# A one-core decoder layer on Trainium2: TensorE's loop order, second SBUF buffers, matmuls ahead of the first weights, and new orders on every engine

## The reference

```python
# 16 heads of 16, 64 random features (orf)
phi(z)  = (exp(z @ orf.T / 2 - |z|^2 / 8) + 1e-6) / 8
a       = phi(q) @ (phi(k).T @ v) / (phi(q) @ sum(phi(k)))       # linear attention, q, k, v from x
x1      = LN(x + a @ Wo.T + bo)
x2      = LN(x1 + softmax(q' k'.T / 4) v')                       # q' from x1, k', v' from the context
gate,up = aq(x2) @ tern(w_gate).T, aq(x2) @ tern(w_up).T         # aq: rows rounded to 8 bits
out     = LN(x2 + aq(silu(gate) * up) @ tern(w_down).T)          # tern: weights rounded to three levels
```

## Time and profile before

| | us |
|---|---|
| median of 3 runs | 495.16 (495.1 to 498.17) |
| the profiled execution, its own time | 495.66 |
| its span, first to last instruction | 493.6 |
| PE busy | 447.2 (91% of the span) |
| DVE busy | 436.0 (88%) |
| ACT busy | 429.1 (87%) |
| POOL busy | 393.3 (80%) |
| mean granted clock of TensorE | 0.977 of full |

### The profile page before, as it was taken

One profiled execution on the slowest core, in us unless ns is written; L12 is line 12 of the kernel. 1 busy time (PEld: TensorE's weight loads), 2 busy tenths in 40 slices (PEclk: granted clock), 3 DMA queues, 4 the chain that ended last, 5 costly groups with the idle time before them and its releaser, 6 DMA issues.

```text
span 493.6 us, 18532 instructions
## 1 busy us (share of the span) xinstructions
PE 447.2 (91%) x6598; PEld 305.1 (62%) x6598; DVE 436.0 (88%) x1286; ACT 429.1 (87%) x879; POOL 393.3 (80%) x885
## 2 busy tenths in 40 slices
PE   5588898999999999999999999999999999878752
PEld 3345666777666766777767677766766666554321
DVE  7755568999999999999999999999999999898771
ACT  3398988999999999999999999999999999776632
POOL 3379677889997898999999999999999897764533
PEclk9889999999999999999999999999999999997997
DMA  7848667777787587566666666666667676542122
GB/s 206 263 109 140 124 120 110 132 134 140 142 142 140 121 150 143 116 140 148 140 142 139 143 143 139 144 149 149 145 130 136 118 140 141 97 76 56 42 55 64
DMA packets 192660, 64.27 MB, mean 130 GB/s; under 512 B 172385, under 2 KB 192353, under 8 KB 192609
## 3 DMA queue, kind: packets, MB, share of 16 engines
q1 hardware_dynamic: 192432, 63.60, 64.2%
q10 hardware_dynamic: 176, 0.01, 0.0%
HBM read 17.31 MB, written 4.19 MB: 44 GB/s over the span
## 4 chain that ended last, share of the span: by engine, by line
PE 58%; DMA 11%; ACT 10%; DVE 9%; issue 5%; POOL 3%; SPq 3%; POOLq 0%; DVEq 0%; ACTq 0%
PE bank L1355 10%; PE bank L1741 8%; DMA tT<-pkT 5%; PE bank L1682 4%; PE bank L1543 4%; PE bank L1780 4%; PE bank L1453 3%; PE bank L1500 2%; PE bank L1719 2%; PE bank L1387 2%; PE bank L1392 2%; DVE hh L1101 2%; DMA pkAT<-pkA 2%; PE bank L1515 2%; PE bank L1571 2%
## 5 line engine op out<-in xcount | busy, mean ns | idle before, releaser
L1355 PE MATMUL bank<-wq_hi,xT 128*128 128x512 f16 (+1 forms) x256 | 73.2, 341 | 1.5 <-ACT xT L636 1.5
L516 POOL TENSOR_TENSOR rs<-ve,mhalf 128x1 f32<-128x1 f32 x96 | 53.2, 555 | 0.0
L1052 DVE TENSOR_REDUCE negm<-bank 128x4 f16<-128x512 f32 x64 | 42.9, 670 | 6.7 <-PE bank L1592 6.6
L1097 DVE SCALAR_TENSOR_TENSOR g<-th,bank 128x512 f32<-128x512 f32 x64 | 43.0, 675 | 4.7 <-ACT th L774 3.5
L750 ACT ACTIVATE pT<-bank 128x512 f32<-128x512 f32 x64 | 39.0, 610 | 8.0 <-PE bank L1672 6.9
L1355 PE MATMUL bank<-wq_lo,xT 128*128 128x256 f16 (+1 forms) x128 | 43.5, 340 | 0.0
L1053 DVE TENSOR_REDUCE negm<-bank 128x4 f16<-128x512 f32 x64 | 43.5, 679 | 0.0
L682 ACT ACTIVATE x<-y,nmr,rs 128x256 f32<-128x256 f32 x64 | 39.8, 623 | 3.6 <-DVE y L1158 2.9
L702 ACT ACTIVATE phq<-bank 128x512 f32<-128x512 f32 x64 | 39.7, 637 | 3.2 <-PE bank L1387 3.2
L1101 DVE TENSOR_TENSOR hh<-g,bank 128x512 f32<-128x512 f32 x64 | 42.4, 674 | 0.0
L1780 PE MATMUL bank<-downT,hqT 128*128 128x256 bf16 x256 | 33.2, 273 | 8.1 <-DMA hqT<-hq 8.1
(11 more groups left out here) (186 smaller groups left out, 1570.0 us busy)
## 6 DMA issues: line engine op xcount, KB each, us to landing
xs<-in_x_dram SPq DMA_DIRECT2D x32, 128.0 KB, 2.3
xr<-in_x_dram SPq DMA_DIRECT2D x32, 128.0 KB, 2.3
cs<-in_ctx_dram SPq DMA_DIRECT2D x32, 128.0 KB, 2.2
out_dram<-ot SPq DMA_DIRECT2D x32, 128.0 KB, 2.0
ffn_ld<-in_L_ffn_w_gate_dram SPq DMA_DIRECT2D x1, 1024.0 KB, 8.9
ffn_ld<-in_L_ffn_w_up_dram SPq DMA_DIRECT2D x1, 1024.0 KB, 6.4
ffn_ld<-in_L_ffn_w_down_dram SPq DMA_DIRECT2D x1, 1024.0 KB, 8.4
pkAT<-pkA SPq DMA_TRANSPOSE x64, 3.2
```

The costliest lines, as they stand in the source:

```text
L516: g.tensor_tensor(rs[n - 1][:, :], ve[n - 1][:, :], mhalf[:, :], ALU.pow).then_inc(done[f"pw{n}"], 1)
L1052: v.tensor_reduce(negm[:, 0, cols], even.rearrange("p (c t) -> p c t", c=4), AX, ALU.max, negate=True)
L1097: v.scalar_tensor_tensor(g1[:, n, :], th[:, n, :], 1.0, gate, ALU.add, ALU.mult).then_inc(done[f"gl{n}"], 1)
L1355: last = T.matmul(o, xT[:, 2 * part + c, :], w[:, c, cols], start=(n == 0), stop=(n == 5))
```

## The change

- **Second buffers.** Eleven tiles (`xpk`, `xT`, `qk`, `pkA`, `pkAT`, `phk`, `x1T`, `pkT`, `pkC`, `hq`, `hqT`) get a dimension of two, indexed by parity. To make room `th` and `g1` are laid over `wld`. Waits that guarded the single buffers go: `hi` and `nhi` no longer wait for the transposes of the tile before, `qT`/`kT` no longer for `phq0`/`phk1` of the tile before, `qk_` not for `lo`, `xhi` not for `xTp`.
- **TensorE's loop order and the PSUM banks.** Both are new. `tm` goes to the end of the iteration with lag 4, `kvp` to near its start with lag 3, `phk0`, `phk1`, `ntp` behind `s0`, `wo` between `st0` and `nump`, `u1` beside `u0`. Waits for freed banks follow the new bank table.
- **Matmuls ahead of the weights.** 18 matmuls of 128 x 128 identity by identity before the first weight transposes, and 8 after the second.
- **Orders anew** on SP, POOL, ACT and DVE, in ramp, loop and drain. In the ramp, DVE's first `magnitude` comes after the first `qk_`, `v_` and `nr`; SP issues `w_up` and `w_down` ahead of `x[2]`; SP's loop has `tT_` last, right behind `load_c` and `load_r`. In the drain 43 unread matmuls stand in place of 32. DVE's clears of `pkA`, `pkC`, `pkT` cover only the rows that no step writes.

```diff
-        pkA = sb("pkA", [P, H, 4, 32], F16)
-        pkAT = sb("pkAT", [P, H, P], F16)
+        pkA = sb("pkA", [P, 2, H, 4, 32], F16)
+        pkAT = sb("pkAT", [P, 2, H, P], F16)
...
-        th = sb("th", [P, 2, 512])
-        g1 = sb("g1", [P, 2, 512])
+        th = wld[:, 0:2, :, :].rearrange("p a b d -> p a (b d)")
+        g1 = wld[:, 2:4, :, :].rearrange("p a b d -> p a (b d)")
...
             def qT(t, par):
-                wait_ahead(sp, t, par, ("lo", 0), ("phq0", -1))
+                wait_ahead(sp, t, par, ("nlo", 0))
...
             def nhi(t, par):
-                wait_ahead(pool, t, par, ("nr", 0), landings=(("kT", -1), ("qT", -1),))
+                wait_ahead(pool, t, par, ("nr", 0))
...
             def hi(t, par):
-                wait_moved(act, "kT", t, par, -1)
-                wait_moved(act, "qT", t, par, -1)
+                wait(act, "qk", t)
...
             def qk_(t, par):
                 wait(dve, "qkm", t)
-                wait(dve, "lo", t, -1)
...
+            def keep_busy(count):
+                for _ in range(count):
+                    T.matmul(at_qk[:, 0:P], idh[:, :], idh[:, :], start=True, stop=True)
+
+            keep_busy(18)
             for n in range(3):
                 transpose_weight(n, weight_banks[n])
+                if n == 1:
+                    keep_busy(8)
...
             def st0(t, par):
+                wait_looped(pe, "tlo", t, 1)
                 wait_looped(pe, "xT", t, 6)
```

More of the change, by code:

```diff
@@ L422, in drain @@
[L422 to L431 removed]
+                trail(tT_, i, -232, 25)
@@ L432, in _ @@
+                trail(qT, i, -235, 28)
+                trail(load_c, i, -235, 28)
+                trail(cT_, i, -233, 25)
+                trail(store, i, -226, 19)
+                trail(hqT_, i, -229, 21)
+                trail(load_r, i, -235, 27)
+                trail(row, i, -232, 24)
+                trail(load_x, i, -258, 30)
+                trail(kT, i, -236, 28)
+            run(sp, ramp, iteration, drain, (-219, -131), 18, 30, (-228, -194))
             for par in range(2):
@@ L880, in _ @@
+            run(act, ramp, iteration, drain, (-31, -16), 16, 30, (-20, -7))
         @block.vector
@@ L1285, in _ @@
+            run(dve, ramp, iteration, drain, (-29, -10), 14, 30, (2, 14))
         @block.tensor
@@ new lines, in ramp @@
+                once(ternaries[1], i, -27)
+                lead(dn, i, -23, 3)
+                lead(kvp, i, -29, 9)
+                if i == -25:
+                    pe.wait_ge(done["m1"], 2)
+                once(ternaries[4], i, -25)
+                lead(wo, i, -28, 8)
+                lead(st1, i, -26, 6)
+                lead(st0, i, -26, 6)
+                lead(nump, i, -29, 9)
+                lead(phk1, i, -30, 10)
+                lead(qkm, i, -32, 12)
+                lead(pv1, i, -26, 6)
@@ new lines, in ramp @@
+                lead(pv0, i, -26, 6)
+                lead(s0, i, -27, 7)
+                lead(phk0, i, -30, 10)
+                lead(ntp, i, -29, 9)
+                lead(xqTp, i, -25, 5)
+                once(output_weight, i, -31)
+                lead(oxp, i, -26, 6)
+                if i == -27:
+                    pe.wait_ge(done["nT"], 3)
+                once(ternaries[2], i, -27)
+                lead(phq1, i, -30, 10)
+                lead(phq0, i, -30, 10)
+                lead(s1, i, -27, 7)
@@ L1913, in _ @@
-            run(pe, ramp, iteration, drain, (-50, -12), 14, 30, (-6, 6))
+                trail(pv0, i, -43, 24)
+                trail(vm, i, -48, 30)
+                trail(s0, i, -44, 25)
+                trail(phk0, i, -47, 28)
+                trail(qkm, i, -49, 30)
+                trail(ntp, i, -46, 27)
+                trail(oxp, i, -43, 24)
+                trail(phq1, i, -47, 28)
+                trail(xqTp, i, -42, 23)
+                trail(s1, i, -44, 25)
+                trail(kvs, i, -47, 28)
@@ new lines, in drain @@
+                keep_busy_at(i, -12, 6)
+                trail(kvp, i, -47, 27)
+                trail(dn, i, -41, 21)
+                keep_busy_at(i, -11, 18)
+                keep_busy_at(i, -12, 13)
+                trail(st1, i, -44, 24)
+                trail(st0, i, -44, 24)
+                trail(wo, i, -46, 26)
+                trail(pv1, i, -44, 24)
+                trail(nump, i, -47, 27)
+                trail(xTp, i, -50, 30)
+                trail(phk1, i, -48, 28)
+            run(pe, ramp, iteration, drain, (-33, -19), 14, 30, (-20, -9))
```

1234 lines of the change are left out of this document (577 added, 657 removed), and 10 rows, old and new, of the table done.

## The result

The kernel after takes 503.48 us (median of 3 runs, 502.51 to 506.65), the kernel before 495.16. The ratio is 1.0156, 95% interval [1.0119, 1.0193]: slower by 1.6%, where I had forecast 483.8. The profiled execution took 502.51 us with a span of 500.8, 7.2 above that of before.

What follows compares the result with a forecast made beforehand. Chains of waits were taken to bound ramp and drain, work the loop (PE full, ACT and DVE close behind). -3.5 - 4.5 + 0 - 2.4 - 1 = -11.4 from 495.66 gave 484.3 us, 483.8 as a median; range 475 to 495.

Steps and rivals of the forecast that it cites:

- The start, -3.5: Before tile 0: `qk_` starts right behind its projection, not behind the gate's `magnitude`; -3.5 us, between -5 and 0.
- Second buffers in 20 to 80 us, -4.5: Ramp: the guards of the single `pkA` on DVE and POOL go; 4.5 us gained, a little under half of ACT's idle time.
- the sign "over 90%": Sign that the forecast is right: ACT over 90% busy in 20 to 80 us.
- 80 to 200 us, "nothing": Gain there put at nothing, engines being 95 to 97% busy; term 0, between -3 and +3 for late landings.
- cost nothing visible: Claim on SP's order, `hqT` buffers, aliases, added waits and clears; without cover, a tenth of a microsecond a tile.
- The loop, -2.4: Tile from 12.94 to 12.84 us by changes of shape and the `mTp` wait; over 24 tiles -2.4, between -7 and +7.
- hidden behind PE: In the loop the guards of the single buffers wait under 0.2 us a tile, covered by PE's work.
- the last rival: Changes of shape are no fewer, nine and nine; the 0.05 us a tile go, +1.2, 485.0; half the forecast's chance.
- SP, POOL, the rest: Remaining order changes each lie on an engine behind work it had to await anyway; no visible cost.
- The distance from `tm` to `s0`: Shrinks by 0.68 us, leaving 0.1 to 0.15; holds in the loop, late ramp landings cost up to 0.68 each.
- the slower rival: Loop: `s0` waits for the transpose each tile; at a 4.1 us landing +18 over 24 tiles, 505 us; chance 0.14.
- The drain, -1: After the loop: same chain, distance less 0.68, new orders may use second buffers; -1 us, between -5 and +4.

Runs made afterwards that it cites:

- e12_start: Kernel before with DVE's first magnitude moved from ahead of the first `qk_` to behind the first `nr`; ratio to the kernel before 0.9958.
- e11_guards: Kernel after with the waits of the single `pkA`, `pkAT` and `qk` put back for tiles 1 to 11; ratio to the kernel before 1.0378.
- e14_buffers: Kernel before with second buffers for `pkA`, `pkAT` and `qk` alone, its orders as they were; ratio to the kernel before 0.9977.
- e13_circle: Kernel after with `ya2` ahead of `chi` in POOL's loop and, in SP's ramp, `hqT_` ahead of `qT` and `store` behind `load_r`; ratio to before 1.0012.
- e1_ya2: Kernel after with `ya2` ahead of `chi` in POOL's loop; ratio to the kernel before 1.0077, a tile 12.96 us.
- e16_s0: e13_circle with `s0` behind `phk0` and `ntp` in TensorE's straight ramp, as it stood before; ratio to the kernel before 1.0073.
- e8_nobusy: Kernel after without the 18 and 8 matmuls ahead of the weights; ratio to the kernel before 1.0238.
- e17_split: e13_circle with `load_r` ahead of `row` and `load_c` behind `tT_` in SP's loop; ratio to the kernel before 1.0061, a tile 12.94 us.
- e6_loads: Kernel after with `load_c` and `load_r` ahead of `row` in SP's loop; ratio to the kernel before 1.0144, a tile 13.29 us.
- e5_qT: Kernel after with `qT` behind `hqT_` and `row` in SP's straight ramp, as before; ratio to the kernel before 1.0174.

## Why the prediction was wrong

*The start, -3.5.* Tile 0 was 4.1 us earlier, at 11.7, and its projection ran at twice the pace. Right in place and size; e12_start shows that only about 2 us of such a gain reach the end.

*Second buffers in 20 to 80 us, -4.5.* Start and ramp together gave 5.9 of the 8.0 by tile 7. In the new orders the guards are worth even more than the term (e11_guards: 6.4 us), but the buffers own only half of it: alone they give nothing there (e14_buffers). ACT's share rose hardly, 50.34 us against 50.05; the sign "over 90%" did not come.

*80 to 200 us, "nothing".* This step failed, by 7.8 us from tile 7 to 17, where the range went to +3. I let the gain of the ramp be lost against engines that are full, and bounded the rest by the late landings at `s0`, 0.68 us each. I had read SP's order only for its last entry. What failed, as far as it is known, is that I put the rest of SP's new order under "cost nothing visible": with `qT` ahead of `hqT_` in the ramp, SP's own issue time, 1.25 us a transpose, entered a circle of 13.3 us. Mending it together with `store` gives 3.2 us by the ratios, 2.7 of them between tiles 7 and 17 in the traces (e13_circle against e1_ya2). That is less than half: the other 6.0 us of this stretch, 2.8 in tiles 8 and 9 and 2.5 in tile 12, stay open. The late landings are real, but before had them too, and giving the distance back in the ramp does not help (e16_s0). Part of it may be an early ramp that is lost again, for which my sum has no term; that is not shown, but e8_nobusy and e11_guards reach tile 7 3.6 and 6.4 us later than the kernel after and tile 17 only 1.2 and 4.2 later.

*The loop, -2.4.* The second failed step, +4.2 from tile 17 to 29. Without its stalls TensorE's own order takes 12.7 us against my 12.84. But the order has little part in that: with the second buffers alone the old order takes 12.74 (e14_buffers), with the wait at `mTp` smaller. The sentence that the guards of the single buffers are "hidden behind PE" in the loop was thus wrong, by 0.19 us a tile. And the changes of shape gave nothing, as the last rival had it: nine in both, and in the kernel after `pv1` starts 0.20 us behind the last matmul of `nump`, as `wo` did before. But "SP, POOL, the rest ... each lies on an engine behind work that it had to await anyway" was wrong for `ya2`: `chi` had come between `hq1` and it, 0.6 us, and POOL, 153.70 us busy of 170, was no cover but a piece of the circle (e1_ya2: 0.33 us a tile).

*The distance from `tm` to `s0`, and the slower rival.* I had 0.1 to 0.15 us to spare at a landing of 3.1. That sum was wrong: `s0` never starts less than 0.14 us behind the landing, and SP issues the transpose 1.97 us behind `tm`, no longer 1.85. At 3.1 us `s0` is 0.15 late (e17_split), and at the 3.3 us that the landings take in the mean, 0.34. The rival's place and sign were right. In the kernel after it decided nothing, since the circle through `ya2` was longer (e6_loads): a wait that shows in the profile is worth nothing while a longer circle runs beside it. Once `ya2` stands earlier, it is what keeps the tile at 12.97 in place of 12.70 (e1_ya2).

*The drain, -1.* +1.0 in the profiled execution, at a granted clock of 0.98 from tile 29 on, where the kernel before had 0.94; its four fellows with the same loop and drain had up to +3.9. The sign was wrong; the step behind it was not followed up.

All in all: -3.5 - 4.5 + 0 - 2.4 - 1 became, by stage, -5.9 + 7.8 + 4.2 + 1.0. With two places in the orders put right, `ya2` on POOL and `qT` (with `store`) on SP, the ratio goes from 1.0156 to 1.0012, but the gains of the start and the ramp still pay for losses behind tile 7 that have no cause here.

## What to carry to other kernels

When every engine's order is new, follow for each step what has come to stand ahead of it in its list and who waits for it, and add up the circles across the engines, the queue's issue time among them; a busy share below 100% says nothing on whether an engine is a piece of one. An idle gap is room only for a step that can run then, and a stall is worth its time only if nothing else is as long; the next longest circle is what remains when the longest is cut. A second buffer and the order that uses it are one edit.

## What was not expected of the hardware

- In unrolled code, DMA transposes with an instruction packet beside them landed after up to 5.08 us, those without after 3.52 at most; in the loop there are no such packets. That the one causes the other was not tested.
- A load or two of 128 KB issued close ahead of a transpose moved its landing from 3.1 to 3.4 or 3.5 us in about every second tile; with them ahead of `row` it was 3.1 to 3.3.
- TensorE's clock in the first projection differs from execution to execution, with matmuls ahead of it or without (2 of 15 and 4 of 5 at 1.2 GHz).
- One kernel's executions scatter by several microseconds (499.7 to 506.2 for e5_qT), while the loop's tile repeats within 0.04 us over the five profiled kernels that share it (13.29 to 13.33).
